# A four-layer graph network: one-hot windows of 32 target nodes per 512 edges in place of 64 per 1024

## The chip, the cores and the metric

The kernel runs on one core of a Trainium2 chip. The metric is the device time of one execution in microseconds (us); smaller is better.

## What is computed

Four graph layers run one after the other on 625 nodes of 512 features and 20,000 edges: a mean aggregation (layer 0), four transformer blocks with attention over the edges (layer 1), a weighted graph convolution (layer 2) and an edge network (layer 3). The change touches how layers 0 to 2 count edges between nodes, and how layer 3 adds messages up:

```python
def _L3_gnn_ref(x, edge_index, edge_attr, W1, b1, W2, b2, W3, b3, W4, b4, gamma, beta):
    src, dst = (edge_index[0], edge_index[1])
    edge_feat = jnp.concatenate([x[src], x[dst], edge_attr], axis=-1)
    h = mish(edge_feat @ W1 + b1)
    messages = mish(h @ W2 + b2)
    agg = jax.ops.segment_sum(messages, dst, num_segments=x.shape[0])
    u = mish(jnp.concatenate([x, agg], axis=-1) @ W3 + b3)
```

The edges are inputs, and they come sorted by target:

```python
src = jax.random.randint(jax.random.fold_in(_gk, 2), (20000,), 0, 625, jnp.int32)
dst = jnp.minimum((625 * jax.random.uniform(jax.random.fold_in(_gk, 3), (20000,)) ** 2.0).astype(jnp.int32), 9999)
_o = jnp.argsort(dst, stable=True)
src = src[_o]
dst = dst[_o]
```

Low nodes have many edges and high nodes few. These are the first target and the span (last target less first) of the last ten groups of 512 edges, as `setup_inputs` draws them with its own seed 0. The largest span of a group before these is 28 (group 32), and the largest span of 1024 edges in a row, counted from an even group, is 59 (groups 36 and 37).

```text
group    30   31   32   33   34   35   36   37   38   39
first   368  391  418  446  473  501  531  562  590  622
span     23   27   28   27   28   30   31   28   32    2
```

## The kernel before, in words

**Groups.** The 20,000 edges are cut into 40 groups of 512 (four tiles of 128 edges); the last group holds 32 edges. Both parts below work on a window of `WIN` = 64 target nodes per group. `SHARE` = 2 groups have one window start, the first target of the two. If some span reaches `WIN`, one pass over the edges does not see every target, and the whole pass is done again with all windows moved on by `WIN`. `k.sweeps` is the number of such further passes: a row of multiples of `WIN` is compared with the largest span (L577), and the hits are added up (L578). `starts` is a table with one start per pass and group (L571 to L579).

**front()** counts edges. Per group DVE compares the source of each edge with all 640 nodes (L607, three tiles; ACT makes the fourth with L371 and L374) and its target with the 64 of the window (L599); POOL multiplies the latter with two weights (L350); PE multiplies source rows by these 3 x 64 = 192 columns, 20 matmuls per group (L491), over two groups into the same PSUM banks; DVE adds them into `sums` at the window's start (L627). The loop runs `n * 10 + 10` turns of four groups, with n = `k.sweeps` (L480). DVE reads a start from the table into a register before it can issue L599 or L627 (L593).

**transformer_and_gcn()** follows and does not depend on the edges' order.

**edge_layer()** works on pairs of tiles, two pairs per group, in a software pipeline; `run_steps` (L1655) unrolls 16 pairs, loops over `n * 20 + 15` turns of four, and unrolls the end. A pair is gathered by POOL's indirect DMAs from two tables (L1756, L1787), turned and given its attribute part by PE (L1861 to L1870), goes through Mish on ACT and DVE, through W2 on PE in 24 matmuls of 512 columns (L223, `edge_z2p`), and through Mish again. Once per group PE adds the messages up by target: the one-hot tile (L2107) is the stationary operand and the messages are the moving one (L1901). As the window fills only 64 columns of the array, the 512 features are two sides of 256 in two column tiles, one above the other in PSUM. DVE copies the sums out (L2131), and POOL adds them into `agg` in DRAM by an accumulating DMA (L1801), 64 rows of 2 x 256. The last four groups go another way (L1885, L2125, L2172): their sums stay on the chip.

The order of work on each engine is that of the code; queues and semaphores do the rest.

## Time and profile before

| | |
|---|---|
| median of 3 runs | 1642.54 us (1638.32 to 1642.61) |
| the profiled execution | 1639.68 us, of which the span shown is 1638.0 us |
| front loop | 16.6 to 104 us |
| transformer and layer 2 | to about 865 us |
| edge loop | 910 to about 1591 us |
| end | to 1638 us |

The profile is of one execution. "Busy" is the time in which an engine works on an instruction; a matmul's end is modelled, so that two in a row can overlap. PEld is the load of the stationary operand. A name with q (DVEq) is the engine's sequencer, which reads registers, waits and issues. Where an engine is busy 99% of a stretch and waits for nothing, it sets the time of that stretch.

### The profile page before, as it was taken

The page shows a single profiled execution, that of the slowest core. Times are in us where ns is not written, and L with a number is a line of the kernel's source. Part 1 is how long each engine was busy: PE and PEld are TensorE (multiplying, and loading weights), DVE is VectorE, ACT ScalarE, POOL GpSimd, SP SyncE. Part 2 cuts the span into 40 slices and gives each one's busy share as a digit, 9 for nine tenths or more (in the row PEclk, how much of TensorE's full clock was granted, in tenths as well). Part 3 has the DMA queues.
Part 4 walks back from the last instruction along what each step waited for, and adds up shares of the span by engine and source line. Part 5 has one row for each costly group of instructions (what it writes and reads, how often), then busy time and mean ns, then how long its engine had stood idle before and what let it go on. Part 6 is the DMA issues. An engine that isn't in the chain of part 4 may idle for free. (4 is left out here: it accounts for less than half of the span.)

```text
span 1638.0 us, 25185 instructions
## 1 busy us (share of the span) xinstructions
PE 1549.4 (95%) x8530; PEld 1226.5 (75%) x8530; DVE 1193.1 (73%) x1976; ACT 1097.3 (67%) x1534; POOL 672.7 (41%) x498
## 2 busy tenths in 40 slices
PE   5789899999999999999999999999999999999987
PEld 4765586878788878877854778787878787888774
DVE  8977646555565646465623499999999999999967
ACT  9841546544554546444530599999999999999963
POOL 3410200120012001200302788888888888888601
PEclk9999899999999999999999999999999999999989
DMA  3001320022012201212106767777777777777710
GB/s 106 0 20 66 92 83 26 15 68 87 26 33 84 77 1 33 81 36 78 41 1 222 160 142 148 146 150 150 148 152 148 152 150 148 149 149 150 170 39 32
DMA packets 107048, 153.95 MB, mean 94 GB/s; under 512 B 42043, under 2 KB 47035, under 8 KB 106467
## 3 DMA queue, kind: packets, MB, share of 16 engines
q0 software_dynamic: 72832, 87.84, 28.4%
q1 hardware_dynamic: 34146, 65.21, 12.6%
q8 instruction: 41, 0.67, 0.2%
q14 instruction: 29, 0.23, 0.0%
HBM read 141.02 MB, written 11.73 MB: 93 GB/s over the span
## 5 line engine op out<-in xcount | busy, mean ns | idle before, releaser
L1787 POOL DMA_INDIRECT edge_gathered<-dst_table,edge_index x158 | 262.0, 1658 | 58.7 <-issue 54.4
L223 PE MATMUL edge_z2p<-edge_w_hi,edge_h_hi 128*128 128x512 f32 x628 | 253.3, 403 | 2.6 <-DVE edge_late L2117 2.6
L223 PE MATMUL edge_z2p<-edge_w_lo,edge_h_hi 128*128 128x512 f32 x628 | 249.0, 396 | 0.0
L223 PE MATMUL edge_z2p<-edge_w_hi,edge_h_lo 128*128 128x512 f32 x628 | 248.8, 396 | 0.0
L1756 POOL DMA_INDIRECT edge_gathered<-src_table,edge_index x158 | 201.8, 1277 | 85.4 <-POOL edge_index L1750 30.6
L977 POOL TENSOR_TENSOR h<-h,tr_row_b 128x512 f32<-128x512 f32 x40 | 59.3, 1520 | 271.4 <-ACT C L1222 271.1
L966 POOL TENSOR_TENSOR tr_cw<-w_c,tr_cw 32x1024 fp32r<-32x1024 f32 x7 | 16.6, 2375 | 348.7 <-ACT tr_cw L1182 348.7
L223 PEld LDWEIGHTS edge_z2p<-edge_w_hi,edge_h_hi 128*128 128x128 f32 x628 | 118.4, 189 | 42.0 <-issue 16.9
L223 PEld LDWEIGHTS edge_z2p<-edge_w_hi,edge_h_lo 128*128 128x128 f32 x628 | 118.5, 189 | 28.5
L223 PEld LDWEIGHTS edge_z2p<-edge_w_lo,edge_h_hi 128*128 128x128 f32 x628 | 118.5, 189 | 25.0
L2134 DVE SCALAR_TENSOR_TENSOR edge_early<-edge_early,edge_z1p 128x1024 f32<-128x1024 f32 x79 | 96.4, 1220 | 48.9 <-ACT edge_early L2002 48.8
L993 PE MATMUL tr_one<-tr_yT_hi,tr_w_hi 128*128 128x256 f32 (+2 forms) x384 | 119.5, 311 | 4.4 <-issue 4.3
L993 PE MATMUL tr_one<-tr_yT_lo,tr_w_hi 128*128 128x256 f32 (+2 forms) x384 | 118.7, 309 | 0.0
L993 PE MATMUL tr_one<-tr_yT_hi,tr_w_lo 128*128 128x256 f32 (+2 forms) x384 | 118.7, 309 | 0.0
L1277 ACT ACTIVATE hT<-hT,tr_nmax 128x626 f32<-128x626 f32 x56 | 45.7, 817 | 95.3 <-DVE tr_nmax L1461 94.6
L2117 DVE TENSOR_TENSOR edge_late<-edge_z2p,w_c 128x512 f32<-128x512 f32 x157 | 101.7, 682 | 9.3 <-PE edge_z2p L223 5.0
L1998 ACT ACTIVATE edge_early<-edge_early 128x1024 f32<-128x1024 f32 x79 | 83.8, 1061 | 27.1 <-DVE edge_early L2090 26.9
L2145 DVE TENSOR_TENSOR edge_h_lo<-edge_early,edge_h_hi 128x1024 fp32r<-128x1024 f32 x79 | 96.8, 1225 | 2.7
L1075 PE MATMUL tr_two<-tr_kT,tr_qT 128*128 128x313 f32 x320 | 98.3, 433 | 0.2
L2097 DVE SCALAR_TENSOR_TENSOR edge_late<-edge_late 128x1024 f32<-128x1024 f32 x79 | 95.7, 1212 | 0.3 <-ACT edge_late L2011 0.3
L1461 DVE CUSTOM_DVE_ANT_0 hT<-tr_two,logc 128x626 f32<-128x626 f32 x80 | 64.6, 807 | 36.2 <-PE tr_two L1075 36.0
L2014 ACT ACTIVATE edge_late<-edge_late 128x1024 f32<-128x1024 f32 x79 | 84.0, 1063 | 4.6 <-DVE edge_late L2137 1.9
(366 smaller groups left out, 4020.0 us busy)
## 6 DMA issues: line engine op xcount, KB each, us to landing
w_c<-in_attr_T SPq DMA_DIRECT2D x78, 128.0 KB, 4.1
agg<-edge_sum_rows POOLq DMA_DIRECT2D x36, 128.0 KB, 10.7
w_a<-in_wv SPq DMA_DIRECT2D x4, 1024.0 KB, 5.3
w_b<-in_wq SPq DMA_DIRECT2D x4, 1024.0 KB, 5.4
w_a<-in_wk SPq DMA_DIRECT2D x4, 1024.0 KB, 7.7
w_b<-in_wo SPq DMA_DIRECT2D x4, 1024.0 KB, 6.8
w_a<-in_m SPq DMA_DIRECT2D x4, 1024.0 KB, 5.4
w_b<-in_m SPq DMA_DIRECT2D x4, 1024.0 KB, 5.5
```

The source lines that it names most:

```text
L223: mm = pe.matmul(out, a, b, start=(n == 0), stop=(n == last))
L993: mm = pe.matmul(out, a, b, start=(start and n == 0), stop=(stop and n == len(terms) - 1))
L1075: mm = pe.matmul(bank[:, f, 0:PART_A], qT[:, h, i * P:(i + 1) * P], kT[:, h, f * PART_A:(f + 1) * PART_A], start=True, stop=True)
L1461: ins = dve.tensor_tensor_reduce(out=cols(scores[n % 2][:, 0:USED], PART_A), in0=bank[:, :, 0:PART_A], in1=cols(k.logc[:, i, 0:USED], PART ...
L1756: pool.indirect_dma_start(out=from_rows[a][:, j, :].bitcast(F32), out_offset=None, in_=k.src_table, in_offset=bass.IndirectOffsetOnAxis(ap ...
L1787: pool.indirect_dma_start(out=from_rows[ring][:, j, :].bitcast(F32), out_offset=None, in_=k.dst_table, in_offset=bass.IndirectOffsetOnAxis ...
L1998: act.activation(m1[one], m1[one], ACT.Square).then_inc(S["inner1_ready"], 1)
L2014: act.activation(m2[two], m2[two], ACT.Square).then_inc(S["square2_ready"], 1)
L2097: dve.scalar_tensor_tensor(h2[new], m2[new], 0.5, z2[new], ALU.subtract, ALU.mult).then_inc(S["h2_ready"], 1)
L2117: dve.tensor_tensor(z2[two][:, j * D:(j + 1) * D], ps_z2[:, j * D:(j + 1) * D], b2, ALU.add).then_inc(S["z2_ready"], 1)
L2134: dve.scalar_tensor_tensor(m1[one], m1[one], 0.5, ps_z1[one][:, :], ALU.subtract, ALU.mult).then_inc(S["h1_ready"], 1)
L2145: dve.tensor_tensor(h1_lo[one][:, :, :], cols(m1[one], EDGE), h1_hi[one][:, :, :].bitcast(F32), ALU.subtract).then_inc(S["lo_ready"], 1)
```

## The change

`WIN` is 32 and `SHARE` is 1: each group of 512 edges has a window of its own, 32 nodes wide. The test for a further pass is the same one with the new `WIN` and the new spans. `SIDES` = 4: a message sum is four column tiles of 128 features in place of two of 256. In front() a group has 96 columns in place of 192, PSUM is added into `sums` after each group, and the table of starts is made by one addition over 800 elements in place of ten small ones. The table is no longer kept between the parts; `first_dst` is, and edge_layer() makes the table anew. (`PLANES` only says which matmul opens and closes a PSUM bank.)

```diff
-SHARE = 2
+SHARE = 1
 SPANS = GROUPS // SHARE
-WIN = 64
+WIN = 32
+SIDES = P // WIN
+PLANES = D // (4 * WIN)
 WIDE = NP + WIN
 MAXSWEEPS = NP // WIN
...
-                for w in range(MAXSWEEPS):
-                    own(dve.tensor_scalar(cols(wtab[:, w * GROUPS:(w + 1) * GROUPS], SHARE),
-                                          shared[:, 0, :, None].to_broadcast([1, SPANS, SHARE]), float(WIN * w),
-                                          float(NP), ALU.add, ALU.min))
-                own(dve.tensor_reduce(span1[:, 0:1], shared[:, 1, :], AX.X, ALU.max))
+                spans = [1, MAXSWEEPS, GROUPS]
+                own(dve.tensor_tensor(wtab[:, 0:MAXSWEEPS * GROUPS].rearrange("p (w g) -> p w g", g=GROUPS),
+                                      iota16[0:1, 0:NP:WIN][:, :, None].to_broadcast(spans),
+                                      k.first_dst[:, None, :].to_broadcast(spans), ALU.add))
+                own(dve.tensor_reduce(span1[:, 0:1], shared[:, :], AX.X, ALU.max))
                 own.wait()
                 step(dve.tensor_scalar(over[:, :], iota16[0:1, WIN:NP:WIN], span1[:, 0:1], None, ALU.is_le))
                 step(dve.tensor_reduce(span1[:, 1:2], over[:, :], AX.X, ALU.add))
-                dve.tensor_copy(k.starts[:, :], wtab[:, :]).then_inc(windows_known, 1)
+                dve.tensor_scalar(starts[:, :], wtab[:, :], float(NP), None, ALU.min).then_inc(windows_known, 1)
                 dve.tensor_copy(k.sweeps[:, :], span1[:, 1:2]).then_inc(windows_known, 1)
...
+                pool.wait_ge(S["last_ready"], 1)
                 pool.wait_ge(dst_stored, 16 * NT)
...
-                        pool.dma_start(k.agg[bass.ds(start, WIN), :].rearrange("n (s c) -> s n c", s=2),
+                        pool.dma_start(k.agg[bass.ds(start, WIN), :].rearrange("n (s c) -> s n c", s=SIDES),
                                        sum_rows[slot][:, :], accum_op=ALU.add).then_inc(sum_stored, 16)
...
-                                for side in range(2):
-                                    mm = pe.matmul(ps_sum[slot][side * WIN:(side + 1) * WIN, 0:D // 2],
+                                for side in range(SIDES):
+                                    mm = pe.matmul(ps_sum[slot][side * WIN:(side + 1) * WIN, 0:D // SIDES],
                                                    onehot[slot][:, b * PT + j, :],
-                                                   h2[b][:, j * D + side * (D // 2):j * D + (side + 1) * (D // 2)],
+                                                   h2[b][:, j * D + side * (D // SIDES):j * D + (side + 1) * (D // SIDES)],
                                                    start=(b == 0 and j == 0), stop=(b == 1 and j == PT - 1))
...
                 own(dve.tensor_copy(iota[:, :], iota_i[:, :]))
+                own(dve.memset(wtab[:, :], 0.0))
+                own.wait()
+                spans = [1, MAXSWEEPS, GROUPS]
+                own(dve.tensor_tensor(wtab[:, 0:MAXSWEEPS * GROUPS].rearrange("p (w g) -> p w g", g=GROUPS),
+                                      iota[0:1, 0:NP:WIN][:, :, None].to_broadcast(spans),
+                                      k.first_dst[:, None, :].to_broadcast(spans), ALU.add))
+                own.wait()
+                dve.tensor_scalar(starts[:, :], wtab[:, :], float(NP), None, ALU.min).then_inc(S["last_ready"], 1)
```

On DVE in front(), where the table and the number of further passes are made, there stands before (`front_over` is the row of hits, `sweeps` their sum):

```order
L572 TENSOR_SCALAR front_wtab<-front_shared 1x40 [waits front_vec]
L572 TENSOR_SCALAR front_wtab<-front_shared 1x40 x9
L575 TENSOR_REDUCE front_span<-front_shared 1x1
L577 TENSOR_SCALAR front_over<-front_iota,front_span 1x9 [waits front_vec]
L578 TENSOR_REDUCE front_span<-front_over 1x1 [waits front_vec]
L579 CAST starts<-front_wtab 1x440 [waits front_vec]
L580 CAST sweeps<-front_span 1x1
```

and in the changed kernel:

```order
L576 TENSOR_TENSOR front_own_part<-front_iota,first_dst 1x800 [waits front_vec]
L579 TENSOR_REDUCE front_span<-front_shared 1x1
L581 TENSOR_SCALAR front_over<-front_iota,front_span 1x19 [waits front_vec]
L582 TENSOR_REDUCE front_span<-front_over 1x1 [waits front_vec]
L583 TENSOR_SCALAR front_starts<-front_own_part 1x840 [waits front_vec]
L584 CAST sweeps<-front_span 1x1
```

The comparison stays where it was and now has 19 multiples of 32 in place of 9 multiples of 64; the two long table instructions stand around it.

In the front loop DVE's queue had, for two groups, two loads of a start and then two comparisons and one addition (ISA are register steps; six L607 follow):

```order
L593 TENSOR_LOAD starts
L593 ISA x3
L593 TENSOR_LOAD starts
L593 ISA x2
L635 REGISTER_ALU
L599 ISA [waits front_group_ready]
L599 TENSOR_TENSOR front_to_onehot<-front_iota,front_dst 128x4x64
L599 ISA
L599 TENSOR_TENSOR front_to_onehot<-front_iota,front_dst 128x4x64
L625 REGISTER_ALU
L627 ISA [waits front_added]
L627 TENSOR_TENSOR front_sums<-front_sums,front_sum_ps 128x15x64
```

and now has, for each single group (three L611 follow):

```order
L597 TENSOR_LOAD front_starts
L597 ISA x3
L597 TENSOR_LOAD front_starts
L597 ISA x2
L639 REGISTER_ALU
L603 ISA [waits front_group_ready]
L603 TENSOR_TENSOR front_to_onehot<-front_iota,front_dst 128x4x32
L629 REGISTER_ALU
L631 ISA [waits front_added]
L631 TENSOR_TENSOR front_sums<-front_sums,front_sum_ps 128x15x32
```

The two loads and their register steps thus come twice as often, and the tiles behind them are half as large.

On PE in the edge loop the message sum of a group stands between the attribute part of a pair and the W2 product of another:

```order
L1869 MATMUL edge_z1p0<-edge_attr_parts0,edge_attr_w_both 128x256
L1870 MATMUL edge_z1p0<-edge_attr_parts0,edge_attr_w_rest 128x256
L1901 MATMUL edge_sump1<-edge_late,edge_onehot1 64x256 x8
L223 MATMUL edge_z2p<-edge_w2_hi,edge_h1_hi0 128x512
L223 MATMUL edge_z2p<-edge_w2_lo,edge_h1_hi0 128x512
```

and now:

```order
L1875 MATMUL edge_z1p0<-edge_attr_parts0,edge_attr_w_both 128x256
L1876 MATMUL edge_z1p0<-edge_attr_parts0,edge_attr_w_rest 128x256
L1907 MATMUL edge_sump1<-edge_late,edge_onehot1 32x128 x16
L225 MATMUL edge_z2p<-edge_w2_hi,edge_h1_hi0 128x512
L225 MATMUL edge_z2p<-edge_w2_lo,edge_h1_hi0 128x512
```

Nothing else moves there: eight sums of 64 x 256 become sixteen of 32 x 128. The chip runs each of these in two instructions, since they are float32.

## Rows read from the trace of the kernel before

**Rows 1.** The page: busy time by engine, and 40 slices of the span.
```profile
PE 1549.4 (95%) x8530; PEld 1226.5 (75%) x8530; DVE 1193.1 (73%) x1976; ACT 1097.3 (67%) x1534; POOL 672.7 (41%) x498
...
PE   5789899999999999999999999999999999999987
...
DVE  8977646555565646465623499999999999999967
ACT  9841546544554546444530599999999999999963
```

**Rows 2.** Stages: us, then busy time and instructions of each engine, clock, DMA.
```profile
16.60:104.00 87.40, 70.70 (x800) 66.31 (x800) 84.91 (x172) 67.53 (x107) 39.94 (x39) 1.00 0.01 5
104.00:860.00 756.00, 721.74 (x3621) 570.69 (x3622) 438.41 (x874) 362.30 (x740) 84.09 (x52) 0.99 0.16 51
...
960.00:1500.00 540.00, 539.34 (x3114) 434.66 (x3113) 496.48 (x649) 515.50 (x519) 444.35 (x322) 1.00 0.76 149
```

**Rows 3.** Instructions by line, over the span: gathers, and register loads of the number of passes.
```profile
L1756 POOL DMA_INDIRECT edge_gathered<-src_table,edge_index x158: 942/1080/2097, 884.4 to 1532.1; - x158
...
L310 DVEq TENSOR_LOAD <-sweeps x1: 550/550/550, 12.8 to 12.8; - x1
```

**Rows 4.** PE's message sums in order of time: the first, one in the middle, the last.
```profile
956.93 1.95 PE L1901 MATMUL edge_sump<-edge_late,edge_onehot 128*64 128x256 f32 x16
...
1205.75 1.95 PE L1901 MATMUL edge_sump<-edge_late,edge_onehot 128*64 128x256 f32 x16
...
1541.12 1.95 PE L1901 MATMUL edge_sump<-edge_late,edge_onehot 128*64 128x256 f32 x16
```

**Rows 5.** DVE in the front loop in order of time, one turn of two groups and the next.
```profile
78.19 0.75 DVE L599 TENSOR_TENSOR front_to_onehot<-front_iota,front_dst 128x256 f16 x2
78.86 1.14 DVE L627 TENSOR_TENSOR front_sums<-front_sums,front_sum_ps 128x960 f32 x1
79.93 2.68 DVE L607 TENSOR_SCALAR front_from_onehot<-front_iota,front_src_f 128x640 f16<-128x640 f16 x6
82.53 0.41 DVE L599 TENSOR_TENSOR front_to_onehot<-front_iota,front_dst 128x256 f16 x1
```

**Rows 6.** DVE's sequencer, 77.2 to 82.5 us, by line: ns min/median/max, first and last start.
```profile
L593 DVEq FUSED_REGOPS  x3: 57/190/190, 78.8 to 79.6; - x3
L593 DVEq TENSOR_LOAD <-starts x2: 311/312/314, 78.5 to 79.2; - x2
L593 DVEq SEQ_ASSERT  x2: 23/23/23, 79.1 to 79.8; - x2
...
L607 DVEq FUSED_REGOPS  x12: 46/57/64, 77.3 to 82.3; - x12
...
L599 DVEq FUSED_REGOPS  x2: 131/133/135, 81.0 to 81.2; - x2
```

**Rows 7.** PE in order of time: sides of other widths, for the price of one matmul.
```profile
897.76 2.32 PE L223 MATMUL edge_sump<-hT,logc 128*128 128x320 f32 x8
...
1203.96 0.80 PE L1861 MATMUL edge_z1p<-edge_ident_r,edge_gathered 128*128 128x128 f32 x8
...
1207.63 0.50 PE L223 MATMUL edge_z2p<-edge_w_hi,edge_h_hi 128*128 128x512 f32 x1
```

**Rows 8.** POOL in the edge loop in order of time.
```profile
1202.36 2.35 POOL L1801 DMA_DIRECT2D agg<-edge_sum_rows  x1
1205.01 1.47 POOL L1756 DMA_INDIRECT edge_gathered<-src_table,edge_index  x1 [0.30 <-PE edge_z1p L1861]
1206.78 0.98 POOL L1756 DMA_INDIRECT edge_gathered<-src_table,edge_index  x1 [0.30 <-DMA edge_gathered<-dst_table,edge_index]
1208.07 1.64 POOL L1787 DMA_INDIRECT edge_gathered<-dst_table,edge_index  x1 [0.30 <-issue]
```

**Rows 9.** DVE in order of time: table building in front, and the start of the edge layer.
```profile
7.98 0.98 DVE L572 TENSOR_SCALAR front_wtab<-front_shared 1x40 f32<-1x40 f32 x10
...
9.51 0.38 DVE L579 CAST starts<-front_wtab 1x440 int32<-1x440 f32 x1
...
903.24 0.43 DVE L2084 CAST edge_attr_parts<-w_c 128x512 fp32r<-128x512 f32 x1 [2.83 <-DMA w_c<-in_attr_T]
```

More of the change, by code:

```diff
@@ L493, in _ @@
                                                to_onehot[a][:, j, :, :].rearrange("p a b -> p (a b)"),
-                                               start=(first and j == 0 and i % 2 == 0), stop=(last and j == TPG - 1 and (i % 2 == 1 or i == NT - 1)))
+                                               start=(first and j == 0 and i % PLANES == 0),
+                                               stop=(last and j == TPG - 1 and (i % PLANES == PLANES - 1 or i == NT - 1)))
                         mm.then_inc(group_ready, 1)
@@ L1586, in edge_layer @@
         onehot = [sb(f"onehot{a}", [P, TPG, WIN]) for a in range(2)]
-        sum_rows = [sb(f"sum_rows{a}", [P, D // 2]) for a in range(2)]
+        sum_rows = [sb(f"sum_rows{a}", [P, D // SIDES]) for a in range(2)]
         own_part = sb("own_part", [P, KF, NP])
@@ L2098, in step @@
                     if a % 2 == 0 and on(6):
-                        start = dve.value_load(k.starts[0:1, bass.ds(g(6), 1)], min_val=0, max_val=NP)
+                        start = dve.value_load(starts[0:1, bass.ds(g(6), 1)], min_val=0, max_val=NP)
                         shape = [P, TPG, WIN]
                         if is_late and is_late(6) == LATE:
-                            dve.wait_ge(S["last_ready"], 2)
+                            dve.wait_ge(S["last_ready"], 3)
                             targets = last_dst[:, :]
@@ L2166, in add_late @@
                 def add_late(w, n):
-                    start = dve.value_load(k.starts[0:1, bass.ds(n * GROUPS + (GROUPS - LATE + w), 1)], min_val=0, max_val=NP)
+                    start = dve.value_load(starts[0:1, bass.ds(n * GROUPS + (GROUPS - LATE + w), 1)], min_val=0, max_val=NP)
                     into = aggT[:, :, bass.ds(start, WIN)]
```

23 lines of the change are left out of this document (13 added, 10 removed).

## The prediction, made before the changed kernel was run

> **What bounds the kernel now.** I read the page first: in its 40 slices PE is busy nine tenths or more in nearly all of them, and DVE and ACT fill up in two places only, at the start and in the last two fifths [rows 1]. The table by stages says what these are. From 16.6 to 104 us, the front loop, DVE is busy 84.9 of 87.4 us and PE 70.7: DVE sets the time. From 960 to 1500 us, in the edge loop, PE is busy 539.3 of 540 us, ACT 515.5, DVE 496.5 and POOL 444.4 [rows 2]: PE sets the time, and ACT stands only 4.5% behind. Between them lies the transformer, which the change doesn't touch.
>
> Both loops run over all edges, and the number of such passes is read from the data. In the profile it was one: POOL's source gather ran 158 times, which is 79 pairs of two tiles, one pass over 40 groups less the empty half of the last one; DVE had loaded the number of further passes at 12.8 us, before either loop [rows 3]. The pace of the edge loop comes from PE's message sums, one per group of 512 edges: the first starts at 956.93 us and the 36th at 1541.12 us [rows 4], so a group takes 584.2 / 35 = 16.69 us. The pace of the front loop comes from two successive starts of L599, 78.19 and 82.53 us [rows 5]: 4.34 us for two groups, 2.17 us each, 86.8 us for 40.
>
> **The number of passes.** This decides everything else. The kernel makes a further pass if a multiple of WIN is less than or equal to the largest span, where span is last target less first. Before, the smallest multiple is 64 and the largest span of 1024 edges 59: none. After, the smallest multiple is 32, and group 38 has targets 590 to 622, span 32. The comparison is "32 is at most 32": true. 64 isn't. So one further pass is made. It isn't a slip of the test: a window that begins at 590 ends at 621, and target 622 lies outside it. But it is for one group of 40 that both loops run over all 40 again, with windows that begin 32 further on and meet hardly any edge. Nothing in the loops is shorter for a window without hits.
>
> **Edge loop, second pass.** 40 more groups at 16.69 us [rows 4] are 667.6 us. They stand inside the loop, so neither the filling nor the end of the pipeline comes twice.
>
> **Front loop.** Per group the change removes half of L599, half of the addition L627 (960 elements once per two groups become 480 once per group) and adds nothing to L607. On DVE itself I get for one group about 0.25 us (from 0.41 for the whole one), 1.14 / 2 + 0.07 = 0.64 us and 2.68 / 2 = 1.34 us [rows 5]; the last holds a stall of the first L607 behind POOL's L350, which is half as long afterwards, so that 1.34 may fall towards 1.0. That makes 1.9 to 2.2 us. But DVE's sequencer must load two starts per group where it loaded two per pair of groups. The two loads start at 78.5 and 79.2 us [rows 6], 0.72 us apart with their register steps, so 1.44 us per group. The rest of its work for two groups runs from the first L599 step at 81.0 us to the last L607 step at 82.3 us [rows 6], 1.3 us or 1.4 with that step; half of it, and some 0.2 us for a wait, the addition's step and the branch, which aren't halved, is 0.9 us. Together 2.35 us, which is more than the engine needs: the sequencer becomes the bound. Ends: 2.0 us (engine bound, loads hidden) and 2.6 us (each wait adds to the chain). I take 2.35, since the loads come in rows at fixed length. Both passes: 80 x 2.35 = 188 us for 86.8 before, +101 us; ends +73 and +121. PE needed 70.7 / 40 = 1.8 us per group before and needs no more after, ACT at most 67.5 / 40 = 1.7 us [rows 2]: both are hidden behind 2.35.
>
> **The message sum on PE.** Before, 16 instructions of 256 columns take from 1205.75 to 1207.63 us [rows 4, 7], 0.117 us each. A float32 matmul of 320 columns on the whole array takes 2.32 / 8 = 0.29 us, 0.27 without its tail [rows 7], so 256 columns alone would be 0.21: the two column tiles do run at once. After, 32 instructions of 128 columns. If four tiles run at once, they cost 32 x 0.117 / 4 = 0.94 us, a gain of 0.94. If each start costs what it does in L1861, 8 in 0.80 us with the tail, 0.08 without [rows 7], they cost 32 x 0.08 = 2.56 us, a loss of 0.68. I take 1.2 us, a gain of 0.7 us, nearer to the same instruction's own row than to a transpose's. Of this gain little arrives. ACT's need is 515.5 / 540 x 16.69 = 15.9 us of a group [rows 2], and POOL shows no rest at all: each gather stands 0.3 us behind the one before, and L1801 takes 2.35 us of it, for 128 pieces before and after (64 x 2, then 32 x 4) [rows 8]. As POOL is released by PE there (L1861), its real slack can't be read. I take 0.3 us per group; ends 0.75 (all but ACT's bound) and -0.68. In two passes 76 groups have such a sum (all but the last four): -23 us; ends -57 and +52.
>
> By the Trainium skill ("TensorE: Matmul & The Clock Gate", the section on 56 against 53.3 ns) starts of matmuls never stand closer than about 25 ns, and about 62 ns where the sequencer's microcode decodes them. No run here shows which. By the second figure 32 starts would take an estimated 1.98 us, about what 16 take now, the sum per group would gain nothing, and the forecast would stand at 2412 us.
>
> **Small parts.** The table in front: 0.98 + 0.38 us are replaced by an addition over 800 elements and a minimum over 840 [rows 9], by the width of L627 and L579 about 1.0 + 0.7 us; +0.4 us ahead of the loop, and one compare less before the first L599. In edge_layer the same table is made again with a memset, 2 to 2.5 us on DVE, in front of L2084, which waited 2.83 us for a DMA [rows 9]: hidden, and 2 us if that DMA comes sooner. POOL's new wait for the table stands where it waits for the tables in DRAM anyway. DVE's L2107 and L2131 are halved, off the path. I take 1 us for all.
>
> **Sum.** 1638.0 + 667.6 + 101 - 23 + 1 = 2384.6 us of span. The profiled execution was 1.7 us longer than its span, and the median of the runs 2.9 us above that: 2389 us.
>
> **The rivals.**
> - *One pass* (the other side). If the inputs on the chip are drawn so that no group spans 32, say last target 621 in group 38, the loops run once. Point of decision: the largest span, 31 or 32; 31 is the next largest (group 36), so a single node decides it. Then front costs 40 x (2.35 - 2.17) = +7 us and 36 sums give 36 x 0.3 = 11 us: 1642.5 + 7 - 11 + 1 = 1640 us, no change to be told; with the full 0.75 us per group 1624 us, faster. For it speaks only that the draw may depend on the generator's version; against it, the span is computed from the reference itself. Chance 0.06, half of it faster.
> - *Two passes, and the sum gets dearer.* The 32 short instructions are bound by their starts, and PE stays the bound, so all of it shows: 76 x 0.68 = 52 us in place of -23, so 2464 us. Against it speaks that column tiles overlap already. Chance 0.07.
> - *Two passes, and PE's gain arrives.* POOL and ACT follow: 76 x 0.75 = 57 us, 2355 us. ACT at 95% speaks against. Chance 0.15.
> - *Forecast:* two passes, small gain on the sums, 2389 us. Chance 0.72.
>
> **How the numbers follow.** Front's ends move the time by -28 and +20, the sum's by -34 and +75. Together low ends give 2327, high ends 2484; both at once are unlikely. The range 2335 to 2440 holds the forecast and the third rival and leaves out about 2 in 10: one pass and the dear sum among them. A measurement tells 0.3%, about 5 us, from no change. Slower 0.94; within 0.3% 0.03; faster 0.03.
>
> **What would show it.** Right: L1756 runs 318 times (159 pairs), L491's matmuls 1600 times for 800, and the transformer's stage is as long as before, but begins about 100 us later. The front loop: starts of the half-size L599 every 2.3 to 2.4 us, with DVE idle between. The edge loop: 16 to 16.7 us from one message sum to the next, 32 instructions each, in about 1.2 us. Wrong: 158 gathers, and then all of this is the wrong question; or a pace of the edge loop above 16.7 us, and then I look at the starts of the short matmuls first and at POOL's L1801 next.

## The result, and the profile after

| | before | after |
|---|---|---|
| median of the runs | 1640.64 us (1638.32 to 1642.61, 4 runs) | 2395.27 us (2395.09 to 2396.51, 4 runs) |
| ratio after / before | | 1.4611, 95% interval 1.4592 to 1.4631 |
| span of the profiled execution | 1638.0 us | 2393.7 us |
| POOL's source gathers (L1756, after: L1761) | 158 | 318 |

The predicted 2389 us and its range (2335 to 2440) hold. The medians below count every execution; the ratios and intervals leave out four that stood far off, one of four of e7 (2658.09 us) and three of ten of e8 (1698 to 1704 us). The kernel makes a second pass over all groups in both loops. First the page of the kernel after: busy time by engine, PE, DVE and clock in 40 slices, and two lines of the chain that ended last (by engine, by line).

```profile
PE 2222.9 (93%) x14386; PEld 1790.7 (75%) x14386; DVE 1853.7 (77%) x2990; ACT 1793.1 (75%) x2254; POOL 1218.4 (51%) x938
...
PE   4668899999999999999999999999999999999997
...
DVE  8887655565556554389899998999999998999986
...
PEclk8668899999999999999999999999999999999998
...
POOL 24%; issue 21%; DMA 4%; PE 4%; POOLq 3%; DVE 2%; ACT 1%; DVEq 0%
```

Against [rows 1]: the stretch at the left, with PE half busy, is twice as long, and the nearly full one at the right, which is the edge loop, has become twice as long too. The largest parts of the chain are POOL's and "issue" now, and PE's granted clock stands at 0.6 of full speed in two slices of the front loop. The table by stages (columns as in [rows 2]: us, then busy time and instructions of PE, PEld, DVE, ACT, POOL, clock, DMA share, GB/s):

```profile
16.60:203.50 186.90, 125.85 (x1596) 113.08 (x1593) 156.33 (x394) 130.30 (x186) 48.22 (x79) 0.65 0.00 1
203.50:960.00 756.50, 719.75 (x3622) 568.42 (x3622) 440.09 (x875) 362.75 (x741) 84.07 (x52) 0.99 0.16 51
...
1060.00:2290.00 1230.00, 1191.67 (x8312) 978.91 (x8311) 1114.92 (x1487) 1178.44 (x1189) 1012.22 (x741) 1.00 0.73 147
```

The first line is the front loop: 1596 of the predicted 1600 matmuls (some records are missing), 186.9 us for the 87.4 of [rows 2]. The second is the transformer, as long as before. In the third, the edge loop, PE is busy 97% of the time, where it was 99.9%; ACT is at 96% and POOL at 82%. Lines from the order of time on PE (start, duration, line, what it writes and reads, count, and in brackets idle time and what ended it): the first message sum, one in the middle with the matmul behind it, the last.

```profile
1054.38 1.08 PE L1907 MATMUL edge_sump<-edge_late,edge_onehot 128*32 128x128 f32 x32
...
1501.76 1.08 PE L1907 MATMUL edge_sump<-edge_late,edge_onehot 128*32 128x128 f32 x32 [0.43 <-DVE edge_late L2113]
1502.77 0.50 PE L225 MATMUL edge_z2p<-edge_w_hi,edge_h_hi 128*128 128x512 f32 x1
...
2297.52 1.08 PE L1907 MATMUL edge_sump<-edge_late,edge_onehot 128*32 128x128 f32 x32
```

76 sums, (2297.52 - 1054.38) / 75 = 16.575 us from one to the next, against 16.69 [rows 4]. The sum itself takes 1501.76 to 1502.77 = 1.01 us against 1.88 [rows 4, 7]. So PE gained 0.87 us per group and the loop 0.12. The bracket shows part of the rest: PE now waits 0.43 us for DVE ahead of the sum.

The extra 755.7 us of span, by those starts: up to the first sum 1054.4 - 956.9 = +97.5; from the first to the last counted sum 1243.1 - 584.2 = +658.9; behind it -0.7, the end of the kernel. Front loop and second pass are all of it.

### The profile page after: what moved, and what is told of

It reads as the page before. It is cut to its first block, busy times and chain, and to the rows that moved or that the text cites. A ratio compares the mean times of both kernels' runs of the same rounds, so it can differ in the third digit from the quotient of the medians.

```text
span 2393.7 us, 43303 instructions
## 1 busy us (share of the span) xinstructions
PE 2222.9 (93%) x14386; PEld 1790.7 (75%) x14386; DVE 1853.7 (77%) x2990; ACT 1793.1 (75%) x2254; POOL 1218.4 (51%) x938
## 4 chain that ended last, share of the span: by engine, by line
POOL 24%; issue 21%; DMA 4%; PE 4%; POOLq 3%; DVE 2%; ACT 1%; DVEq 0%
POOL edge_gathered L1793 12%; POOL edge_gathered L1761 6%; DMA edge_gathered<-dst_table,edge_index 4%; POOL edge_index L1755 4%; POOL agg L1807 3%; PE edge_z2p L225 2%; POOLq L1804 2%; PE edge_z1p L225 1%; PE edge_sump L1891 0%; POOLq L1755 0%; PE edge_sump L225 0%; POOLq L1790 0%; POOLq L166 0%; POOLq L1807 0%; DVE h L2238 0%
## 5 line engine op out<-in xcount | busy, mean ns | idle before, releaser
L1793 POOL DMA_INDIRECT edge_gathered<-dst_table,edge_index x318 | 511.4, 1608 | 108.2 <-issue 96.0
L225 PE MATMUL edge_z2p<-edge_w_hi,edge_h_hi 128*128 128x512 f32 x1268 | 517.7, 408 | 9.7 <-DVE edge_late L2133 3.7
L225 PE MATMUL edge_z2p<-edge_w_hi,edge_h_lo 128*128 128x512 f32 x1268 | 501.7, 396 | 0.0
L225 PE MATMUL edge_z2p<-edge_w_lo,edge_h_hi 128*128 128x512 f32 x1268 | 501.4, 395 | 0.0
L1761 POOL DMA_INDIRECT edge_gathered<-src_table,edge_index x318 | 383.4, 1206 | 154.1 <-issue 67.7
L225 PEld LDWEIGHTS edge_z2p<-edge_w_hi,edge_h_lo 128*128 128x128 f32 x1268 | 238.4, 188 | 57.3
L225 PEld LDWEIGHTS edge_z2p<-edge_w_lo,edge_h_hi 128*128 128x128 f32 x1268 | 238.6, 188 | 50.3
L2004 ACT ACTIVATE edge_early<-edge_early 128x1024 f32<-128x1024 f32 x159 | 168.1, 1057 | 50.3 <-issue 35.2
L2161 DVE TENSOR_TENSOR edge_h_lo<-edge_early,edge_h_hi 128x1024 fp32r<-128x1024 f32 x159 | 194.9, 1226 | 5.5
L2113 DVE SCALAR_TENSOR_TENSOR edge_late<-edge_late 128x1024 f32<-128x1024 f32 x159 | 195.4, 1229 | 0.4 <-ACT edge_late L2017 0.3
L970 POOL TENSOR_TENSOR tr_cw<-w_c,tr_cw 32x1024 fp32r<-32x1024 f32 x7 | 16.7, 2379 | 348.2 <-ACT tr_cw L1186 348.2
L2008 ACT ACTIVATE edge_early<-edge_early 128x1024 f32<-128x1024 f32 x159 | 168.6, 1060 | 5.1
L2006 ACT ACTIVATE edge_early<-edge_early 128x1024 f32<-128x1024 f32 x159 | 168.3, 1059 | 5.0
L1875 PE MATMUL edge_z1p<-edge_attr_parts,edge_attr_w_both 128*128 128x256 f32 x636 | 169.5, 299 | 0.9 <-DVE edge_attr_parts L2169 0.9
L2020 ACT ACTIVATE edge_late<-edge_late 128x1024 f32<-128x1024 f32 x159 | 169.2, 1064 | 0.9 <-issue 0.9
L2014 ACT ACTIVATE edge_late<-edge_late 128x1024 f32<-128x1024 f32 x159 | 166.0, 1044 | 3.4 <-DVE edge_late L2133 3.4
L2001 ACT ACTIVATE edge_late<-edge_late 128x1024 f32<-128x1024 f32 x159 | 167.1, 1051 | 0.1
L2017 ACT ACTIVATE edge_late<-edge_late 128x1024 f32<-128x1024 f32 x159 | 166.2, 1046 | 0.0
```

The source lines that it names most:

```text
L225: mm = pe.matmul(out, a, b, start=(n == 0), stop=(n == last))
L1761: pool.indirect_dma_start(out=from_rows[a][:, j, :].bitcast(F32), out_offset=None, in_=k.src_table, in_offset=bass.IndirectOffsetOnAxis(ap ...
L1793: pool.indirect_dma_start(out=from_rows[ring][:, j, :].bitcast(F32), out_offset=None, in_=k.dst_table, in_offset=bass.IndirectOffsetOnAxis ...
L1875: pe.matmul(z1[:, c, :], attr_w_both[:, chunk], attr_parts[slot][:, pair], start=False, stop=False)
L2004: act.activation(m1[one], m1[one], ACT.Square).then_inc(S["inner1_ready"], 1)
L2006: act.activation(m1[one], m1[one], ACT.Ln, bias=1.0).then_inc(S["inner1_ready"], 1)
```

## The experiments

Each stands by its edit and is called by the number in its name (e1 is e1_w32_one_pass). The code is cut: semaphore increments at the ends of lines and unchanged lines are left out. "Pace" is the time from one message sum on PE to the next, (last - first start) / 35 for one pass, read as above; where the text gives it for single groups, it says so. For the front loop, "us per group" is the same average over DVE's adds (L627, after: L631). All paces are of the one profiled execution, the times are medians of all.

**Is it the number of passes?** Two runs: the narrow windows with one pass, and the old windows with two.

```
-  dve.tensor_copy(k.sweeps[:, :], span1[:, 1:2])
+  dve.tensor_scalar(k.sweeps[:, :], span1[:, 1:2], 0.0, None, ALU.mult)
```

> The changed kernel with the number of further passes set to 0. It leaves out the edges of group 38 whose target is node 622, in the counts and in the message sums, and nothing else. If the second pass is the whole loss: 1638 + 40 x (2.30 - 2.17) = +5 us in front and -36 x 0.12 = -4 us in the edge loop (16.57 us per group in the changed kernel's trace, 16.69 before), so 1641 us, within 8 us of the kernel before. Rival, the narrow windows themselves cost (short matmuls, more register loads, smaller DMA pieces): well over 1700 us.

e1: 1636.48 us (10 runs), ratio to before 0.9987 (0.9977 to 0.9996). Span 1628.9 us. The sums start at 960.5 us (before 956.9), pace 16.40 us. The profiled execution (1630.52 us) is the fastest of the ten, so how often this kernel keeps that pace isn't known.

```
-  dve.tensor_copy(k.sweeps[:, :], span1[:, 1:2])
+  dve.tensor_scalar(k.sweeps[:, :], span1[:, 1:2], 1.0, None, ALU.add)
```

> The kernel before with the number of further passes set to 1; its result is complete, since the second windows meet no edge that the first have counted. If a pass costs its instructions whatever its windows meet: 1640.6 + 40 x 16.69 (667.6) + 40 x 2.17 (86.8) = 2395 us, the same as the changed kernel within 10 us. Rival, the second pass is dear only with narrow windows: clearly below 2350 us.

e2: 2395.56 us (4 runs), ratio 1.4612 (1.459 to 1.4635): to 0.3 us the time of the changed kernel. The chain of this kernel, by engine, is PE's, where that of the changed kernel is POOL's:

```profile
PE 56%; DVE 2%; ACT 1%; issue 1%; DMA 0%; DVEq 0%; POOLq 0%; POOL 0%
```

So the whole loss is the second pass, and the rest of the change is worth nothing in two passes. Why nothing: the first sum starts at 1044.6 us here and at 1054.4 us in the changed kernel (front loop 2.14 us per group against 2.31), the pace is 16.705 us against 16.575, and 75 x 0.13 us give back the 9.8 us that were lost up to the first sum.

**Narrow windows without the second pass.** The front loop stays as it was; the edge loop has windows of 32 nodes per group, but 64 for the last four groups, whose sums take another way (L1891), and counts its passes by itself. The result is complete.

```
+  # span of the last four groups counts 32 less
+  dve.tensor_scalar(espan[:, GROUPS - LATE:GROUPS], espan[:, GROUPS - LATE:GROUPS], float(WIN - EWIN), None, ALU.subtract)
+  dve.tensor_scalar(eover[:, :], iota16[0:1, EWIN:NP:EWIN], espan1[:, 0:1], None, ALU.is_le)
-  pe.matmul(ps_sum[slot][side * WIN:(side + 1) * WIN, 0:D // 2], onehot[slot][:, b * PT + j, :], ...
+  pe.matmul(ps_sum[slot][side * EWIN:(side + 1) * EWIN, 0:D // ESIDES], onehot[slot][:, b * PT + j, 0:EWIN], ...
```

> Complete result, one pass. Front loop as before (64 nodes, one window for two groups). Edge loop with 32 nodes per group, but the last four groups, whose sums stay on the chip, with 64, and a pass count of its own; the largest span of groups 0 to 35 is 31. If POOL's chain of gathers takes over when PE's message sum gets shorter, a group takes 16.57 us as in the changed kernel: 1640.6 - 36 x 0.12 = 1636 us, a gain of 4 us, hardly told. Rival, PE stays the bound and its whole gain of 0.88 us per group (1.88 to 1.0) arrives in one pass: 1609 us.

e3: 1632.54 us (5 runs), ratio 0.9955 (0.9941 to 0.9968), so a little faster than the kernel before. The pace was 16.53 us in all, and it isn't even. The first three sums:

```profile
959.98 1.08 PE L1919 MATMUL edge_sump<-edge_late,edge_onehot 128*32 128x128 f32 x32
975.70 1.08 PE L1919 MATMUL edge_sump<-edge_late,edge_onehot 128*32 128x128 f32 x32
991.42 1.08 PE L1919 MATMUL edge_sump<-edge_late,edge_onehot 128*32 128x128 f32 x32
```

The first two groups take 15.72 us each, and from the fourth on nearly all take 16.56 to 16.59. The expectation of e9 below speaks of "16.39 us per group at first, then 16.57": that took the average of the first quarter, these two fast groups included, for a pace. There was none of 16.39 us in e3. Its chain is POOL's in the edge loop, where e1's, with 16.39 us in nearly every group, is made of ACT, DVE and "issue". (Here too one execution speaks for all: e3's profiled one, 1636.35 us, is the slowest of its five.)

**What holds the edge loop at 16.4 or 16.57 us?** In e1 ACT is busy 552 of 570 us (960 to 1530 us), and POOL, with the 0.3 us between its gathers, has little rest. So one of them was made shorter, then both, all on e1.

```
-  pool.dma_start(k.agg[bass.ds(start, WIN), :].rearrange("n (s c) -> s n c", s=SIDES), sum_rows[slot][:, :], accum_op=ALU.add)
+  pool.dma_start(k.agg[bass.ds(start, 1), 0:D // SIDES], sum_rows[slot][0:1, :], accum_op=ALU.add)
```

> The kernel of e1_w32_one_pass (the changed kernel held at one pass, 16.40 us from one message sum to the next, 1636.5 us), and in addition the adding transfer that POOL issues for each group is cut from 128 rows of 512 bytes (POOL busy 1.58 us on it in e1_w32_one_pass) to one row. It leaves out nearly all message sums of groups 0 to 35, and the edges of group 38 that one pass leaves out. Theory: with the sum made cheap on PE, the edge loop is set by ACT, which in e1_w32_one_pass is busy 552.4 of the 570.0 us from 960 to 1530 us and waits only 0.35 us of each group, for DVE. Then nothing moves: 16.40 us per group, 1634 to 1639 us. Rival: POOL's own order of gathers, index copy and adding transfer sets it, as the chain of waits of the changed kernel says of its second pass. POOL is busy 448.9 of the 570 us; a shorter transfer takes off 0.5 to 0.9 us per group until ACT's 16.0 us bind: 16.0 to 16.1 us per group, 1621 to 1626 us.

e4: 1638.54 us (10 runs), ratio 1.0 (0.9991 to 1.001), pace 16.55 us, and 16.55 in nearly every group. Neither: the pace rose, and the transfer of one row still held POOL for 1.47 us against 1.58 (e1) and 1.85 (e5) for 128 rows. So this edit took away only 0.1 to 0.4 us and says little on POOL as the bound.

```
-  act.activation(m2[old], m2[old], ACT.Ln, bias=1.0)
+  act.activation(m2[old][:, 0:64], m2[old][:, 0:64], ACT.Ln, bias=1.0)
```

> The kernel of e1_w32_one_pass, with one of ACT's sixteen passes per group made short: the first logarithm of the second layer's activation (L2001, 128x1024, 1.05 us, 62 times in 500 us, so twice per group) works on 64 of its 1024 columns. It leaves out the rest of that logarithm, so messages are not the reference's. Theory (ACT sets the loop): ACT gets 2.0 us per group shorter, and the next engine binds, PE, busy 558.3 of 570.0 us, thus at 16.06 us or a little above: 16.06 to 16.2 us per group, 1622 to 1629 us. Rival (POOL or its gathers set it): 16.40 us stays, 1634 to 1639 us. If the wait for the logarithm is part of a ring of DVE, ACT and PE, the gain is the same as in the theory, so this run tells ACT's path from POOL's only.

e5: 1636.97 us (10 runs), ratio 0.9988 (0.9978 to 0.9998), pace 16.52 us: two groups of 15.7 us, then 16.57 as in e3 and in the changed kernel. ACT fell from 552 to 495 us of 570, and the time stayed. So ACT, the busiest engine beside PE, doesn't set the pace of 16.57 us, the changed kernel's. As this loop didn't run at e1's 16.39 us, the run doesn't say whether ACT sets that one.

Then both edits together:

> Both cuts of e4_short_add and e5_short_log in the kernel of e1_w32_one_pass; it leaves out what those two leave out. If PE is next after ACT, this is e5_short_log within 2 us, 16.06 to 16.2 us per group. If POOL is next after ACT (16.2 or 16.3 us in e5_short_log), this run is 0.1 to 0.3 us per group shorter than e5_short_log, 4 to 10 us in all, and only then PE's 16.06 us bind.

e6: 1637.04 us (10 runs), ratio 1.0001 (0.9978 to 1.0023), pace 16.50 us: from the third group on 16.55 us, as in e4, with next to nothing added by the second cut. The chains of e4 and e5 are ACT's and DVE's at 16.55 and 16.57 us, where those of e3 and of the changed kernel are POOL's at 16.57; so the chain doesn't tell what sets the pace here.

The lines of POOL show what differs between e1 and the slower ones. In 1100 to 1500 us (instructions, us busy, mean ns, then idle before and what ended it), first e1, pace 16.40:

```profile
L1793 POOL DMA_INDIRECT edge_gathered<-dst_table,edge_index x98 | 174.1, 1776 | 29.9 <-issue 29.9
L1755 POOL COPY edge_index<-edge_pair_index 128x8 int32 x24 | 15.4, 640 | 11.0 <-PE edge_z1p L1867 11.0
```

then e5, at 16.57 us:

```profile
L1793 POOL DMA_INDIRECT edge_gathered<-dst_table,edge_index x98 | 157.3, 1605 | 29.9 <-issue 29.9
...
L1755 POOL COPY edge_index<-edge_pair_index 128x8 int32 x24 | 42.7, 1780 | 0.0
```

The copy of 128x8 indices, once a group, takes 0.64 us in the one and 1.78 in the other, and only in the first has POOL time left to wait for PE. The changed kernel is of the second kind from its third group on. But the length of the copy doesn't fix the pace. In e4, at 16.55 us, it is 1.13 us (first line), and POOL still has no rest, since its source gathers take 1.45 us each (second line) for 1.20 in e5:

```profile
L1755 POOL COPY edge_index<-edge_pair_index 128x8 int32 x24 | 27.0, 1127 | 0.0
L1761 POOL DMA_INDIRECT edge_gathered<-src_table,edge_index x98 | 141.9, 1448 | 42.3 <-issue 22.1 <-POOL edge_index L1755 20.2
```

And in the kernel before it is 0.82 us for most groups. In the changed kernel POOL's order of time shows the copy, and DVE's shows what ran beside it:

```profile
1505.65 1.77 POOL L1755 COPY edge_index<-edge_pair_index 128x8 int32 x1
1508.24 1.01 POOL L1761 DMA_INDIRECT edge_gathered<-src_table,edge_index  x1 [0.81 <-POOL edge_index L1755]
```

```profile
1505.44 0.69 DVE L2159 CAST edge_h_hi<-edge_early 128x1024 fp32r<-128x1024 f32 x1
1506.17 1.23 DVE L2161 TENSOR_TENSOR edge_h_lo<-edge_early,edge_h_hi 128x1024 fp32r<-128x1024 f32 x1
1507.32 0.42 DVE L2100 CAST edge_attr_parts<-w_c 128x512 fp32r<-128x512 f32 x1
```

The copy begins at 1505.65, while L2159 runs, and ends at 1507.42 us; DVE's L2161, which reads two operands in SBUF, ends at 1507.40. In e1 the copy begins at 1205.83 and ends at 1206.40, with L2113, which began at 1205.14 and ended at 1206.36:

```profile
1205.83 0.57 POOL L1755 COPY edge_index<-edge_pair_index 128x8 int32 x1 [0.52 <-PE edge_z1p L1867]
```

```profile
1205.14 1.22 DVE L2113 SCALAR_TENSOR_TENSOR edge_late<-edge_late 128x1024 f32<-128x1024 f32 x1
```

Both times POOL's copy ends just behind one of DVE's instructions, and so it goes on: 73 of the changed kernel's 80 copies begin in L2159 and end 0.03 to 0.04 us behind L2161, and 35 of e1's 40 end 0.05 us behind L2113. The same copy takes 0.19 us where DVE is idle, ahead of the loop (POOL of e3):

```profile
867.28 0.19 POOL L1767 COPY edge_index<-edge_pair_index 128x8 int32<-128x8 int32 x1 [1.94 <-DVE edge_pair_index L2068]
```

So it waits for DVE. The Trainium skill ("SBUF — State Buffer", "Who interferes with whom" and "SBUF: two separate sides") has a rule for it: DVE and GpSimd share a pair of SBUF ports that one instruction holds to its end, and a DVE instruction with two SBUF operands contends for it with a GpSimd instruction that reads SBUF. By that rule the copy would end just behind DVE's instruction, and the two traces agree: 0.02 and 0.04 us behind in the lines above. What it leaves open is the start: L2159, in which the changed kernel's copy begins, is a cast with one operand and ends 0.04 us before L2161 begins, and yet the copy isn't done by then.

**Take the copy off POOL.** On e3; SP now issues it as a transfer inside SBUF, and POOL waits for that. With the copy go POOL's wait for earlier gathers, which SP takes over, and the 0.8 us that the next gather waited behind the copy.

```
-  pool.tensor_copy(index[a // 2][:, :, :, :], pair).then_inc(S["index_ready"], 1)
+  for lag in (3, 4):   # on SP, behind the attribute loads of the group
+      sp.wait_ge(dst_added[(a - lag) % RING], s(-lag) // RING * (16 * PT) + 16 * PT)
+  sp.dma_start(index[slot][:, :, :, :], pair).then_inc(S["index_ready"], 16)
```

> The kernel of e3_edge32_late64 (32-node windows in the edge loop alone, the last four groups in 64-node windows, one pass; 16.39 us per group at first, then 16.57, 1632.5 us, complete result) with the copy of each group's 128x8 indices taken off POOL (1.78 us busy and 0.81 us of waiting behind it per group in the slow stretch, 0.64 us in the fast stretch of e1_w32_one_pass): SP issues it as a transfer inside SBUF. Theory (the step from 16.39 to 16.57 us is POOL's, whose index copy waits out DVE's work): POOL loses 1.4 to 2.6 us per group, the slow stretch does not come, 16.35 to 16.42 us per group throughout, 5 to 6 us less in all, 1625 to 1629 us. Rival (the two paces are a matter of phase between ACT, DVE and PE, and POOL only follows): both paces stay, 1630 to 1634 us. Rival (the transfer lands late, about 2 us after its issue, and each group's first gather waits for it): 16.7 us per group or more, 1638 us or more.

e9: 1642.7 us (12 runs), ratio 1.0022 (1.0013 to 1.0031). The pace did what the theory said: after some groups of 16.4 to 16.8 us it is 16.40 in nearly every one (e3: 16.57). POOL isn't less busy for it: 474.7 of the 570 us from 960 on, against 468.8 in e3, as its source gathers now take 1.56 us each for 1.20. So the 16.57 us went when the copy went, but the trace doesn't show which part of POOL's work had made them. The time did not follow: everything began late. POOL's first gathers in e3 and in e9:

```profile
886.55 1.60 POOL L1773 DMA_INDIRECT edge_gathered<-src_table,edge_index  x1 [18.65 <-DMA src_table<-edge_late]
```

```profile
909.80 1.23 POOL L1779 DMA_INDIRECT edge_gathered<-src_table,edge_index  x1 [43.05 <-issue]
```

SP issued the first index transfers behind its stores of both node tables, of which the first gather needs only the source table. It cost 23 us there and 13.7 us at the first sum (973.7 for 960.0 us). The last experiment issues these two ahead of the stores:

```
+  for slot in range(2):   # on SP, ahead of the stores of src_table and dst_table
+      sp.dma_start(index[slot][:, :, :, :], pair_index[:, 2 * slot:2 * slot + 2, :, :]).then_inc(S["index_ready"], 16)
```

> The kernel of e9_sp_index, complete result, with the first two index transfers issued by SP before it stores the node tables, not behind them. In e9_sp_index the loop kept 16.40 us per group, but POOL's first gather started at 909.8 us of its span, against 886.6 us in e3_edge32_late64, and the first message sum at 973.7 against 960.0. Theory (the whole loss of e9_sp_index against e3_edge32_late64 is this late start): the first gather starts at 886 to 889 us, the first sum at 960 to 963, 16.40 us per group after it, so 1626 to 1631 us in all, 13 us less than e9_sp_index and 2 to 6 us less than e3_edge32_late64. Rival (SP's waits for the gathers hold up its attribute loads, and cost at the loop's start whatever the first transfers do): the first sum at 965 or later, 1633 to 1643 us.

e12: 1629.26 us (5 runs), ratio 0.995 (0.9933 to 0.9967). The theory holds: first gather at 885.4 us, first sum at 957.3, and 16.40 us per group from the sixth on. It is 13.4 us below e9, and the fastest kernel here with a complete result; against e3 (0.9941 to 0.9968) the intervals overlap, so that they differ isn't shown. DVE and ACT stay as busy as in e1, and POOL is busier (478.0 us, e1 448.9):

```profile
960.00:1530.00 570.00, 556.89 (x3865) 457.42 (x3865) 515.48 (x696) 551.53 (x557) 478.00 (x313) 1.00 0.76 151
```

**How much room has PE?** On e1, all matmuls of the message sum twice, and half the scale at the copy-out.

```
-  for j in range(PT):
+  for again, j in [(x, y) for x in range(2) for y in range(PT)]:
-  dve.tensor_scalar(sum_rows[slot][:, :], ps_sum[slot][:, 0:D // SIDES], -2.0, None, ALU.mult)
+  dve.tensor_scalar(sum_rows[slot][:, :], ps_sum[slot][:, 0:D // SIDES], -1.0, None, ALU.mult)
```

> The kernel of e1_w32_one_pass (16.40 us per group, 1636.5 us) with the 32 instructions of each group's message sum issued twice, both adding into the same PSUM rows, and the copy-out scaled by -1 in place of -2; it leaves out what e1_w32_one_pass leaves out. 32 instructions took 1.0 to 1.1 us in the changed kernel. Theory (in the one-pass loop PE is about 0.3 us per group from being the bound: busy 558.3 of 570.0 us, 16.06 us per group): the first 0.3 us vanish and the rest arrives, 17.0 to 17.2 us per group, 1657 to 1664 us. Rival (the sum stands in a ring in which PE's time counts in full, wherever PE idles): 17.4 to 17.5 us per group, 1672 to 1676 us. Rival (PE has room, the loop is set by POOL at 16.55 us): below 16.7 us, 1642 to 1647 us.

e8: 1639.95 us (10 runs), ratio 1.0006 (0.9995 to 1.0016), pace 16.62 us. Two lines of PE and the table from 960 to 1530 us:

```profile
1208.68 1.95 PE L1907 MATMUL edge_sump<-edge_late,edge_onehot 128*32 128x128 f32 x64
1210.56 0.50 PE L225 MATMUL edge_z2p<-edge_w_hi,edge_h_hi 128*128 128x512 f32 x1
```

```profile
960.00:1530.00 570.00, 569.94 (x4950) 479.71 (x4942) 515.16 (x688) 547.01 (x551) 469.04 (x343) 1.00 0.75 147
```

64 instructions take 1.88 us, to the hundredth what 16 wide ones took in the kernel before, and with the same PE time come nearly the same time and pace. Suppose PE is full here. Take the 1.88 us away from the 16.59 us of nearly every group, and PE's other work is 14.71 us; with a single sum of 1.01 us it is 15.72. The first groups of e3, e5 and e7, in which PE is busy without a break, bear this out: 15.71 to 15.72 us. So the last rival's pace came, below 16.7 us, but with PE full and not with room on it. The theory was wrong by its premise: PE's 558 of 570 us busy in e1 aren't 16.06 us of need per group, the likely reason being that matmuls are pipelined and their ends modelled, so that short waits between them are counted as busy. PE has 0.68 us of room at 16.40 us, not 0.34. The kernel before shows the same: a group took 16.57 to 16.62 us up to the 15th and about 16.70 after it (the last 18.1), with PE busy over 99% in both stretches.

**The front loop.** On e1, the add at a fixed window, so that DVE loads one start per group and not two; then, in a run of its own, both loads kept and one of them placed behind the compare.

```
-  into = sums[:, :, :, bass.ds(start, WIN)]
+  into = sums[:, :, :, 0:WIN]
-  start, start_next = start_of(u), start_of(u + RING)
+  start, start_next = None, start_of(u + RING)
```

> The kernel of e1_w32_one_pass, with one register load less per group on DVE in the first loop: the sums of a group are added at a fixed window of 32 columns, not at the group's own. It leaves out the placing of the node sums, so the result is not the reference's. The edge loop is as in e1_w32_one_pass. Theory (the first loop is paced by DVE's own sequence of loads and address arithmetic: 0.36 us idle to issue before each compare, 2.23 us per group, of which about 1.95 us busy): a load less takes off 0.2 to 0.3 us per group, 8 to 12 us in all, 1624 to 1629 us, and the idle time ahead of L603 shrinks to 0.1 us. Rival (the hand-over between PE and DVE paces it: PE waits 0.8 to 1.2 us per group for DVE's add): 2.20 to 2.25 us per group stay, 1634 to 1639 us.

e7: 1619.79 us (4 runs), ratio 0.9887 (0.9867 to 0.9907). In the front loop 2.23 us per group became 1.81. These averages hold a faster beginning and end; inside the loop a group takes 2.37 us in e1 as in the changed kernel, and 1.89 in e7. DVE is busy 69.56 of the 70 us from 20 to 90 us (e1: 59.40):

```profile
20.00:90.00 70.00, 45.61 (x749) 40.53 (x747) 69.56 (x184) 62.79 (x100) 22.04 (x36) 0.88 0.00 0
```

The theory holds: DVE's sequencer paced the loop, by its loads and register steps, and without one load DVE itself does. A by-product: this kernel's edge loop is line for line that of e1, but from its fourth group on it took 16.57 us per group, where e1 and e11 took 16.39. So 16.57 us needs no change in the loop's own work; what differs is the moment of entering it (first sum at 943.5 us, e1 960.5).

```
-  start, start_next = start_of(u), start_of(u + RING)
+  start_next = start_of(u + RING)
   ...compare_to(u + (RING + b), a + b, start_next)
+  start = start_of(u)
```

> The kernel of e1_w32_one_pass with one line moved: in the first loop DVE's register load of the add's window stands behind the compare instead of ahead of it; as many instructions as before, no other work left out than in e1_w32_one_pass. Theory (0.36 us idle ahead of each compare is the two loads, 0.3 us each, that DVE's sequencer has to get through after the last long instruction; behind the compare one of them is covered): 1.81 to 1.95 us per group in place of 2.23, 11 to 17 us less than e1_w32_one_pass, 1620 to 1626 us. Rival (e7_fixed_add gained by the fixed address of the add, not by the missing load): 2.15 to 2.25 us per group, 1634 to 1639 us.

e11: 1635.07 us (10 runs), ratio 0.9979 (0.9969 to 0.9988), 2.21 us per group, and 2.37 inside the loop as in e1. The theory fails. Two lines of DVE in order of time:

```profile
60.12 0.65 DVE L631 TENSOR_TENSOR front_sums<-front_sums,front_sum_ps 128x480 f32 x1 [0.59 <-issue]
...
61.58 0.28 DVE L603 TENSOR_TENSOR front_to_onehot<-front_iota,front_dst 128x128 f16 x1
```

The idle time moved with the load, from the compare (0.36 us in e1) to the add, and stayed in the sum. That speaks for the sequencer's whole work per group, not its order. The rival's number came, 2.15 to 2.25 us; its reason, the add's address from a register, is small by the rows: L631's register step on DVE's sequencer takes 0.05 us, a load 0.31, and two loads start 0.72 us apart [rows 6]. No run parts the two, as e7 took out the load and the register address together.

The last one puts the same order of loads into e9, with windows of 36 nodes for each group in the front loop.

```
-  to_onehot = [sb(f"to_onehot{a}", [P, TPG, 3, WIN], F16) for a in range(RING)]
+  to_onehot = [sb(f"to_onehot{a}", [P, TPG, 3, FWIN], F16) for a in range(RING)]   # SHARE = 1, FWIN = 36
```

> The kernel of e9_sp_index, complete result, with the first loop in windows of 36 nodes, one for each group (before: 64 nodes for two groups, 2.14 us per group), and DVE's register load for the add placed behind the compare instead of ahead of it. Three column ranges of 36 are 108 columns per matmul; the widest group (33 nodes) fits, so one pass. Theory (with the loads covered, DVE's busy time of 0.29 + 0.65 + 1.21 us less overlap, 1.81 us per group in e7_fixed_add, sets the pace, and 36 in place of 32 columns add 0.05 to 0.1 us): 1.85 to 1.95 us per group, 8 to 12 us less than e9_sp_index. Rival (the add at a window given by a register costs the same wherever its load stands): 2.2 to 2.3 us per group, 3 to 6 us more than e9_sp_index.

e10: 1645.78 us (6 runs), ratio 1.0046 (1.0033 to 1.0059): e9 and 3.1 us more, by 2.22 us per group in the front loop (2.37 inside it, with PE's clock at 0.83 there). Two register loads per group again, and the rival's number came as in e11. Its edge loop, the third without the copy, settled at 16.40 us too.

## Why the prediction was right, point by point

- **Number of passes**: right, and it decided everything. 318 gathers; e1 and e2 show from both sides that the second pass is the loss. The first rival's case was made by force in e1: 1636.5 us, for which it gave 1640, or 1624 with PE's whole gain.
- **Edge loop, second pass**: right. From the first sum to the last, 667.6 us at the old pace, less 75 x 0.116 us for the faster pace, are the 658.9 measured.
- **Front loop**: 2.35 us per group by the sum of the sequencer's loads and steps; measured 2.37 inside the loop and 2.31 over all of it, and +99.5 us at the end of the loop's last add (104.0 to 203.5) for the predicted +101. e7 shows the reason, not only the size: with less on the sequencer, DVE's own need of 1.89 us appears, just under the 1.9 to 2.2 of the working. What the prediction didn't ask about is PE's clock. The granted clock was 1.00 in this loop before [rows 2] and 0.65 after, so the statement that PE "needs no more after" than its 1.8 us per group rested on a clock that didn't stay. It costs little here, since PE is not the bound: inside the loop e10 took 2.37 us at 0.83 as the changed kernel did at 0.65.
- **The message sum on PE**: the guess was 1.2 us (ends 0.94 and 2.56), measured 1.01: close to the end where four tiles run at once, and the nearer row was the right one to lean on. The dear sum of the second rival didn't come. By the Trainium skill's 62 ns for each start where microcode decodes ("TensorE: Matmul & The Clock Gate", "Wait — 56ns, not 53.3ns?") 32 starts were an estimated 1.98 us; 1.01 us is 32 ns each, so that figure doesn't apply here. Nor do the 25 ns that the prediction quotes as the least distance of two starts: on the average they are kept, but the trace has the starts inside a set of four 6 to 7 ns apart.
- **Of this gain little arrives**: right in direction, and the size was off. 0.3 us per group were guessed and 0.116 came, 8.7 us for 23. In one pass the guess fits e1's profiled execution, 16.69 to 16.40, but not e7's, 16.57 in most groups of the same loop; so that fit is partly luck. The step that failed is the bound: the working says of POOL that "its real slack can't be read" and takes the bound from ACT in its place. e5 shows that ACT doesn't set the changed kernel's 16.57 us, and in e9, e10 and e12, with the copy taken off POOL, the loop settles at 16.40.
- **Small parts**: +1 us; in e1, one pass, the front loop's last add ends 4.3 us later than before (108.3 us for 104.0) and the first sum starts 3.6 us later. None of the small parts shows beside that.
- The span came out 9.1 us above the sum's 2384.6: +14.3 for the gain on the sums that didn't arrive, -1.5 for the front loop, and -3.7 for the rest (small parts, the way to the first sum, the end). The median lay 1.6 us above the span, not 4.6, which leaves 6.3 us.

**What stays open.** What holds the edge loop at 16.40 us when PE needs 15.72 and POOL has lost its copy. In e1 DVE waits 46.9 us of 570 for ACT's L2008, and ACT 13.5 us for DVE's L2106, so a ring of these two is the natural suspect; no run took it apart, and none made ACT shorter at this pace. Open too is what in POOL's work makes the 16.57 us, as a copy of 1.13 us (e4) went with 16.55 and POOL stayed as busy without one; why the loop falls into the one pace or the other; and how often each kernel does, as only one execution of each was traced.

## What to carry to other kernels

A change of window, tile or span that has a fallback for data which doesn't fit must be checked against the data before anything else: here one target node in one group of 40 doubled two loops, and the gain inside the loop paid back 9 of the 668 us. When the bound engine is relieved, don't take the rest from another engine's busy share: ACT at 96% did not set the changed kernel's pace (e5), and PE at 98% in e1 had twice the room that this seems to leave (e8). And look at a pace group by group before you average it: two groups of 15.7 us at the start looked like a quarter at 16.39. Last, give exceptions a path of their own (here the last four groups, which had one already) in place of a pass over everything.

## What the runs showed of the hardware

- Four column tiles of 32 do overlap for float32: 32 instructions of 128 columns in 1.01 us, 64 in 1.88, where two tiles of 64 took 1.88 us for 16 of 256 columns.
- A POOL copy of 128x8 indices beside a busy DVE takes 0.64 us (e1), 1.13 (e4) or 1.78 (e7) and ends with one of DVE's instructions; it takes 0.19 where DVE is idle. e1 and e7 have the same edge loop and kept different paces in it, 16.39 and 16.57 us.
- A transfer of one row of 128 elements held POOL for 1.47 us, one of 128 rows of 512 bytes for 1.58 to 1.85, and one of 128 pieces of 1 KB for 2.34 in the kernel before: most of what POOL pays doesn't go with the rows.
- In the front loop PE's granted clock fell to 0.65, with two levels in the rows: 20 matmuls in 1.01 us at 100.95 us of the span and in 1.76 us at 103.19 us, both after waits for DVE's add. In e7, where PE waits less for that add (17.8 us from 20 to 90 us, e1 22.5), it was 0.88 in this stretch, in e1 0.68.

```profile
100.95 1.01 PE L494 MATMUL front_sum_ps<-front_to_onehot,w_c 128*128 128x96 f16 x20 [0.78 <-DVE front_sums L631]
...
103.19 1.76 PE L494 MATMUL front_sum_ps<-front_to_onehot,front_from_onehot 128*128 128x96 f16 x20 [1.23 <-DVE front_sums L631]
```
